# Statistics of a stage taken in the stage before it, and buffers filled one stage early, in an eight-stage kernel

## What is computed

```python
x = x + tanh(g_xattn[0]) * long_convolution(ctx, ctx, layernorm(x))
x = x + tanh(g_ffn[0])   * mixture_of_64_experts(layernorm(x))
x = x + tanh(g_xattn[1]) * rms_attention(layernorm(x), ctx)            # "second attention", 32 heads
x = x + tanh(g_ffn[1])   * mixture_of_8_experts_top_2(layernorm(x))    # "second mixture"
x = x + tanh(g_xattn[2]) * int8_attention(layernorm(x), ctx)           # "quantised attention"
x = x + tanh(g_ffn[2])   * int4_feed_forward(layernorm(x))
x = x + tanh(g_xattn[3]) * causal_attention(layernorm(x), ctx, ctx)
x = x + tanh(g_ffn[3])   * ternary_feed_forward(layernorm(x))
```

## Time and profile before

| | us |
|---|---|
| runs of the kernel before, median of 3 | 2333.38 |
| lowest and highest run | 2327.88, 2338.29 |
| the profiled execution, its own time | 2331.26 |
| its span, first to last instruction | 2329.5 |
| second attention, main loop | about 815 to 911 |
| second mixture | 911 to 1271 |
| quantised attention, first block; scoring loop | 1271 to about 1400; to 2004 |
| quantised feed-forward | 2004 to 2078 |
| causal attention | 2078 to 2227 |
| ternary feed-forward | 2227 to the end |

### The profile page before, as it was taken

How to read it: one execution, slowest core, us unless ns; L and a number is a source line. 1 busy time by engine, 2 the same in 40 slices (tenths; PEclk the granted TensorE clock), 3 DMA queues, 4 the chain that set the end, 5 groups by cost and what they waited for, 6 DMA issues and landing times. The chain is left out here.

```text
span 2329.5 us, 49096 instructions
## 1 busy us (share of the span) xinstructions
PE 1920.9 (82%) x17689; PEld 1096.4 (47%) x17713; DVE 1648.5 (71%) x2772; ACT 1344.6 (58%) x1832; POOL 893.1 (38%) x778
## 2 busy tenths in 40 slices
PE   3875999999997786899997778888888888558855
PEld 1343656656564464468874433333333333334533
DVE  4776765555555556853335889999999999457975
ACT  3444633333334675643332459999999999545566
POOL 4760000000001462500014447888888888334301
PEclk9776999999998898899999865555555555679989
DMA  6334221211222303513223116656666566120100
...
DMA packets 384868, 195.32 MB, mean 84 GB/s; under 512 B 312301, under 2 KB 355311, under 8 KB 382703
## 3 DMA queue, kind: packets, MB, share of 16 engines
...
## 5 line engine op out<-in xcount | busy, mean ns | idle before, releaser
L2455 POOL CAST qa_pT<-qa_eT 128x2048 bf16<-128x2048 uint8 x256 | 477.4, 1893 | 110.6 <-PE qa_OY L2481 95.0
L2568 ACT ACTIVATE qa_e<-qa_scores,qa_nb 128x2048 uint8<-128x2048 f32 x256 | 510.4, 1994 | 4.2
L2578 DVE TENSOR_SCALAR_CACHE_REDUCE qa_scores<-qa_S,qa_sq 128x1024 f32<-128x1024 f32 (+1 forms) x256 | 456.0, 1830 | 4.3 <-PE qa_S L2473 3.4
L2473 PE MATMUL qa_S<-qa_kT,qa_qT 32*128 32x512 f16 x1024 | 373.2, 615 | 95.6 <-DVE qa_scores L2578 94.3
L1116 POOL MEMSET rms_nothing<- 128x512 f16 x1 | 0.5, 524 | 579.8 <-POOLq L3486 579.8
L2473 PEld LDWEIGHTS qa_S<-qa_kT,qa_qT 32*128 32x128 f16 x1024 | 64.6, 108 | 310.2 <-DVE qa_scores L2578 267.0
L973 PE MATMUL moe_G<-hT,moe_W 128*128 (+1 forms) x792 | 193.7, 381 | 7.1 <-DVE moe_zero L941 7.1
L982 PE MATMUL moe_O<-moe_W,moe_ap 128*128 (+1 forms) x1584 | 194.5, 273 | 4.1 <-DVE moe_ap L937 4.1
L913 ACT ACTIVATE moe_ap<-moe_a 128x512 f16<-128x512 f32 x132 | 83.1, 629 | 194.6 <-DVE moe_a L935 194.6
L973 PE MATMUL moe_U<-hT,moe_W 128*128 (+1 forms) x792 | 192.7, 379 | 0.0
L982 PEld LDWEIGHTS moe_O<-moe_W,moe_ap 128*128 128x128 f16 x1584 | 154.7, 98 | 50.3 <-DVE moe_ap L937 3.9
...
## 6 DMA issues: line engine op xcount, KB each, us to landing
...
moe_W<-in_moe_w SPq DMA_DIRECT2D x40, 384.0 KB, 12.1
...
qa_eT<-qa_e SPq DMA_TRANSPOSE x256, 3.1
...
```

Of the source, the lines that this page charges most:

```text
L2455: nc.gpsimd.tensor_copy(pT[:, u % RING, :, :].rearrange("p (b r) q -> p b r q", r=2), pairs).then_inc(s_cast, 1)
L2473: last = nc.tensor.matmul(S[:, banks[i], :], qT[rows, g, t * P:(t + 1) * P], kT[rows, g, parts[i] * QW:(parts[i] + 1) * QW], start=True, s ...
L2568: nc.scalar.activation(e8[:, u % RING, :], scores[:, u % RING, :], ACT.Exp, bias=nb[:, p % 2, i:i + 1], accum_out=sums[:, u:u + 1]).then_i ...
L2578: nc.vector.tensor_scalar(target, S[:, banks[0]:banks[-1] + 1, :], sq[:, t, h:h + 1], so_far, ALU.mult, ALU.max, accum_out=greatest).then_ ...
```

## The change

Two small tiles, `sh.stats` and `sh.mv`, become shared by all stages. (1) The second attention's VectorE loop gets a `bn_aggr` and a `bn_stats` per row tile, for tiles that are finished, and a rest behind the loop; the second mixture starts at its square root. (2) The second mixture's last units get two `bn_stats` and two `bn_aggr` per unit from unit 72 on, and a rest behind `output(3)`; the quantised attention has no statistics of its own, and its four square roots stand first in ScalarE's list. (3) The causal attention's mask and its three stacks are allocated one stage earlier, by a new class, and filled there by GpSimd, which also makes the bf16 mask; ScalarE's copy of the mask and TensorE's waits for them are gone. The causal attention keeps its own statistics.

Two hunks that only declare `sh.stats`, `sh.mv` and a semaphore, and the shortened lists of semaphores, are left out here:

```diff
@@ -1383,6 +1386,14 @@
 
+                def next_statistics(t):
+                    dve.wait_ge(s_res, 2 * t + 2)
+                    nc.vector.bn_stats(sh.stats[:, t, :], sh.X[:, t, :]).then_inc(s_stats, 1)
+
+                def next_moments(t):
+                    dve.wait_ge(s_stats, t + 1)
+                    nc.vector.bn_aggr(sh.mv[:, t, :], sh.stats[:, t, :])
+
                 keys(0)
@@ -1392,7 +1403,14 @@
                     evacuate(t, 1)
+                    if t >= 2:
+                        next_moments(t - 2)
+                    if t:
+                        next_statistics(t - 1)
                 output(NB - 1, 1)
+                next_moments(NB - 2)
+                next_statistics(NB - 1)
+                next_moments(NB - 1)
 
@@ -1543,8 +1559,7 @@
             def _(act):
-                act.wait_ge(s_mv, NB)
-                nc.scalar.activation(std[:, :], mv[:, :, 1], ACT.Sqrt, bias=sh.eps[:, 0:1]).then_inc(s_std, 1)
+                nc.scalar.activation(std[:, :], sh.mv[:, :, 1], ACT.Sqrt, bias=sh.eps[:, 0:1]).then_inc(s_std, 1)
                 act.wait_ge(s_rw, 16)
@@ -1594,11 +1609,6 @@
                 chained = chain_on(dve, s_d)
-                for t in range(NB):
-                    nc.vector.bn_stats(stats[:, t, :], sh.X[:, t, :]).then_inc(s_stats, 1)
-                dve.wait_ge(s_stats, NB)
-                for t in range(NB):
-                    nc.vector.bn_aggr(mv[:, t, :], stats[:, t, :]).then_inc(s_mv, 1)
                 nc.vector.memset(L[:, :, NE:16], LOW)
@@ -1694,8 +1704,17 @@
 
+                def next_statistics(t):
+                    dve.wait_ge(s_comb, NB + t + 1)
+                    dve.wait_ge(s_res, t // 4 + 1)
+                    nc.vector.bn_stats(sh.stats[:, t, :], sh.X[:, t, :]).then_inc(s_stats, 1)
+
+                def next_moments(t):
+                    dve.wait_ge(s_stats, t + 1)
+                    nc.vector.bn_aggr(sh.mv[:, t, :], sh.stats[:, t, :])
+
                 positions()
-                done = 0
+                done, known = 0, 0
                 for i in range(UNITS):
@@ -1717,14 +1736,23 @@
                     if i >= LAST + 4:
+                        ended = min(done - NB, NB - 4)
                         for k in range(done, min(done + 3, 2 * NB)):
...
                         done = min(done + 3, 2 * NB)
+                        for t in range(known, min(known + 2, ended)):
+                            next_statistics(t)
+                            if t:
+                                next_moments(t - 1)
+                            known = t + 1
                 dve.wait_ge(s_D, UNITS)
...
                     combine(k)
-                dve.wait_ge(s_comb, 2 * NB)
+                for t in range(known, NB):
+                    next_statistics(t)
+                    next_moments(t - 1)
+                next_moments(NB - 1)
 
@@ -2218,8 +2244,7 @@
                     def deviations(c):
-                        act.wait_ge(s_mv, (c + 1) * Q)
-                        nc.scalar.activation(std[:, quarter(c)], mv[:, quarter(c), 1], ACT.Sqrt, bias=sh.eps[:, 0:1]).then_inc(s_std, 1)
+                        nc.scalar.activation(std[:, quarter(c)], sh.mv[:, quarter(c), 1], ACT.Sqrt, bias=sh.eps[:, 0:1]).then_inc(s_std, 1)
 
@@ -2252,11 +2277,11 @@
 
+                    for c in range(Q):
+                        deviations(c)
                     weights_high(wk, wkf, s_wk, 16, s_wkhi)
...
                         context_high(c)
-                    for c in range(Q):
-                        deviations(c)
                     weights_high(wv, wvf, s_wv, 32, s_wvhi)
@@ -2280,18 +2305,11 @@
 
-                    def statistics(c):
-                        for t in range(c * Q, (c + 1) * Q):
-                            nc.vector.bn_stats(stats[:, t, :], sh.X[:, t, :]).then_inc(s_stats, 1)
-                        dve.wait_ge(s_stats, (c + 1) * Q)
-                        for t in range(c * Q, (c + 1) * Q):
-                            nc.vector.bn_aggr(mv[:, t, :], stats[:, t, :]).then_inc(s_mv, 1)
-
                     def scales(c):
...
                         dve.wait_ge(s_rstd, c + 1)
-                        nc.vector.scalar_tensor_tensor(out=shift[:, quarter(c)], in0=mv[:, quarter(c), 0], scalar=-1.0, in1=rstd[:, quarter(c)],
+                        nc.vector.scalar_tensor_tensor(out=shift[:, quarter(c)], in0=sh.mv[:, quarter(c), 0], scalar=-1.0, in1=rstd[:, quarter(c)],
                                                        op0=ALU.mult, op1=ALU.mult).then_inc(s_shift, 1)
@@ -2337,10 +2355,7 @@
                     for c in range(Q):
-                        statistics(c)
-                        if c:
-                            scales(c - 1)
-                    scales(Q - 1)
+                        scales(c)
                     for p in range(PAIRS):
@@ -2608,7 +2623,7 @@
 
-def quantised_ffn(nc, sh, weights):
+def quantised_ffn(nc, sh, weights, next_buffers):
 
@@ -2645,6 +2660,7 @@
+                next_buffers.fill(pool)
@@ -2894,7 +2910,43 @@
 
-def causal_attention(nc, sh, a, gate, next_weights):
+class CausalBuffers:
+
+
+    SLOT, CW, NH, HD = 64, 32, 16, 16
+    PARTS = 3 * HD
+
+    def __init__(self, nc, ctx):
+        self.nc = nc
+
+        def sb(n, shape, dt=F32):
+            return ctx.enter_context(nc.sbuf_tensor("ca_" + n, shape, dt))
+
+        self.maskf = sb("maskf", [P, 2, 4, P])
+        self.mask = sb("mask", [P, 2, 4, P], BF16)
+        self.qs = sb("qs", [P, 4, self.NH, self.SLOT], F16)
+        self.ks = sb("ks", [P, 2, self.NH, self.SLOT], F16)
+        self.vx = sb("vx", [P, 4, self.NH, self.CW])
+        self.s_set, self.s_mask = (nc.alloc_semaphore(name="ca_" + n) for n in ("set", "mask"))
+
+    def fill(self, pool):
+        nc, maskf, s_set, s_mask = self.nc, self.maskf, self.s_set, self.s_mask
+        for tile in (maskf[:, :, :, :], self.qs[:, :, :, :], self.ks[:, :, :, :], self.vx[:, :, :, :]):
+            nc.gpsimd.memset(tile, 0.0).then_inc(s_set, 1)
+        pool.wait_ge(s_set, 4)
+
+        nc.gpsimd.affine_select(out=maskf[:, 0, :, :], in_=maskf[:, 0, :, :], compare_op=ALU.is_ge, fill=LOW,
+                                base=0, pattern=[[0, 4], [-1, P]], channel_multiplier=1).then_inc(s_mask, 1)
+
+        nc.gpsimd.affine_select(out=maskf[:, 1, :, :], in_=maskf[:, 1, :, :], compare_op=ALU.is_ge, fill=LOW,
+                                base=0, pattern=[[0, 4], [1, P]], channel_multiplier=-1).then_inc(s_mask, 1)
+        pool.wait_ge(s_mask, 2)
+        nc.gpsimd.tensor_copy(self.mask[:, :, :, :], maskf[:, :, :, :])
+        nc.gpsimd.memset(self.ks[:, :, :, self.PARTS:self.PARTS + 1], 1.0)
+        nc.gpsimd.memset(self.vx[:, :, :, self.HD:self.HD + 1], 1.0)
+
+
+def causal_attention(nc, sh, a, gate, next_weights, buffers):
 
@@ -2918,16 +2970,12 @@
-        maskf = sb("maskf", [P, 2, HALF, P])
-        mask = sb("mask", [P, 2, HALF, P], BF16)
+        mask, qs, ks, vx = buffers.mask, buffers.qs, buffers.ks, buffers.vx
-        qs = sb("qs", [P, 4, NH, SLOT], F16)
-        ks = sb("ks", [P, 2, NH, SLOT], F16)
-        vx = sb("vx", [P, 4, NH, CW])
@@ -2963,19 +3011,6 @@
             def _(pool):
-                nc.gpsimd.memset(maskf[:, :, :, :], 0.0).then_inc(s_set, 1)
-                nc.gpsimd.memset(qs[:, :, :, :], 0.0).then_inc(s_set, 1)
-                nc.gpsimd.memset(ks[:, :, :, :], 0.0).then_inc(s_set, 1)
-                nc.gpsimd.memset(vx[:, :, :, :], 0.0).then_inc(s_set, 1)
-                pool.wait_ge(s_set, 4)
-
-                nc.gpsimd.affine_select(out=maskf[:, 0, :, :], in_=maskf[:, 0, :, :], compare_op=ALU.is_ge, fill=LOW,
-                                        base=0, pattern=[[0, HALF], [-1, P]], channel_multiplier=1).then_inc(s_mask, 1)
-
-                nc.gpsimd.affine_select(out=maskf[:, 1, :, :], in_=maskf[:, 1, :, :], compare_op=ALU.is_ge, fill=LOW,
-                                        base=0, pattern=[[0, HALF], [1, P]], channel_multiplier=-1).then_inc(s_mask, 1)
-                nc.gpsimd.memset(ks[:, :, :, PARTS:PARTS + 1], 1.0).then_inc(s_set, 1)
-                nc.gpsimd.memset(vx[:, :, :, HD:HD + 1], 1.0).then_inc(s_set, 1)
                 for t in range(NB):
@@ -3033,8 +3068,6 @@
                         normalise(2 * c + 1)
-                act.wait_ge(s_mask, 2)
-                nc.scalar.activation(mask[:, :, :, :], maskf[:, :, :, :], ACT.Copy).then_inc(s_mask16, 1)
                 normalise(4)
@@ -3210,8 +3243,6 @@
 
-                pe.wait_ge(s_set, 6)
-                pe.wait_ge(s_mask16, 1)
                 queries_turned(0)
@@ -3514,10 +3545,11 @@
         with own_semaphores(nc):
-            quantised_ffn(nc, sh, quantised)
+            buffers = CausalBuffers(nc, ctx)
+            quantised_ffn(nc, sh, quantised, buffers)
         with own_semaphores(nc):
             ternary = TernaryWeights(nc, ctx, a)
-            causal_attention(nc, sh, a, sh.gates[:, 6:7], ternary)
```

(1 more changed line is left out.)

21 lines of the change are left out of this document (10 added, 11 removed).

## The result

Over 20 runs each the kernel after took 2324.25 us (2318.02 to 2330.65), the kernel before 2331.59 us (2326.38 to 2339.92). The ratio is 0.9962 with a 95% interval of 0.9953 to 0.9972. On 2331.59 us that is 8.9 us less, between 6.5 and 11.0 (the two medians themselves lie 7.3 us apart, inside that). That is a real gain, and it stays under the 0.5% that the prediction named as its bound. The forecast was a sum of -9.25 us and 2323.

What follows compares the result with a forecast made beforehand. No engine bounds the whole: time is the sum of eight barrier-separated stages, each with its own limit. Terms -4.65 - 2.5 - 2.1 = -9.25 us from 2332.3 give 2323 us, range 2315 to 2330.

Steps and rivals of the forecast that it cites:

- the 0.5%: Whole kernel: smallest difference a measurement can tell from no change, about 0.5% (11.7 us); most of the gain below it.
- Seam 1: Second attention to second mixture: start 5.3 us earlier, loop additions free, tail 0.65 us; together -4.65 us.
- rival (d): Second attention's loop: two added operations overrun the 0.75 us cover 15 times; slower, for example +15 us, 2347; chance 0.05.
- Rival (e): Second mixture's start: dense units wait for weight tiles, so the 5.3 us are lost; -4 us, 2328; chance 0.05.
- Seam 2, start: Quantised attention's start: first key product 8.5 us earlier, less waits behind GpSimd; gain 5.5 us (bounds 3.4 and 8.5).
- the eight `keys` follow back to back on VectorE, so the rest slides: Quantised attention's keys: VectorE sets the pace, so the 5.5 us gained at the first carry through.
- my bound of 3.4: Quantised attention's start: gain only 3.4 us if VectorE gets in only when GpSimd's whole run ends.
- Seam 2, end: Second mixture's end: last down product 0.95 us later, 2.0 us behind `output(3)`; together 3.0 us added.
- the 0.27 us a unit: Second mixture's last units: VectorE falls behind 0.27 us per unit over four units, as additions exceed 0.63 us idle time.
- Seam 3, causal attention: Causal attention's start: without fills and mask cuts there, `queries(0)` comes 3.3 us earlier (bounds 2.6 and 4.9).
- Seam 3, fills: Quantised feed-forward's start: GpSimd's fills may hold VectorE's `tensor_scalar`; cost 1.2 us, middle of 0 and 2.4.
- the good bounds of seam 2: Second mixture to quantised attention: with every bound on the good side, stated as -6.8 us; expected -2.5 us.

Runs made afterwards that it cites:

- Experiment 12: Spread fills kernel plus two unread bn_stats per tile in the second attention's loop; 2322.3 us in one execution, the kernel before 2328.2 beside it.
- seam 2 alone: Kernel before, with only the quantised attention's statistics moved into the second mixture's last units; ratio 0.9983 (0.9967 to 0.9999).
- the two pairs above: Changed kernel against seam 2 alone (first scores 106.35, 104.27 us); spread fills against those plus 64 identity transpositions starting the feed-forward (106.05, 99.53).
- experiment 1: Kernel before, with only the second mixture's statistics moved into the second attention's loop (seam 1 alone); ratio 0.9986 (0.9970 to 1.0002).
- set 1: Profiles on one chip: each seam alone on the kernel before (ratios 0.9986, 0.9983, 1.0006), and spread fills on the changed kernel (0.9955).
- experiment 3: Kernel before, with only the causal buffers' fills moved into the quantised feed-forward (seam 3 alone); ratio 1.0006 (0.9987 to 1.0025).
- experiments 5 and 6: Changed kernel with each fill waiting for the one ahead, or with a fifth unread fill; 2337.3 and 2342.8 us in one execution each.
- spread fills: Changed kernel with mask and cuts first, query and key stacks after the first rounding, value stack after the first down products; ratio 0.9955 (0.9941 to 0.9969).

## Why the prediction came out as it did

The total was right, -8.9 for -9.25 us, and two of the three seams did not come about as I had said. That the total fits so closely is luck: two errors cancel (below).

**Seam 1: as predicted.** -5.30 for the start (5.3), +0.68 for the tail (0.65), nothing in the loop (103.1 and 103.0 us). Experiment 12 puts two more `bn_stats` there and still gets no more than 0.2 us out of all 15 tiles; rival (d) was far off. Rival (e) is refuted: the mixture is shorter by the full amount.

**Seam 2, start: the step that failed is "the eight `keys` follow back to back on VectorE, so the rest slides".** Three things were off. First, the gain at `keys(0)` is 6.9 us and not 8.5: I took the end of one tile's product (1282.96) for the end of the pair that VectorE waits for. Second, the holds were mis-sized in the way of my bound of 3.4: the first `tensor_scalar` stood until GpSimd's whole run of low halves had ended, 3.71 us, so that 3.9 us were left (in three later profiles it stood for 1.1 to 1.7 us only). Third, and this is the failed step, VectorE does not bound the keys at the lower clock. There a pair of key products takes TensorE 3.85 us, against 3.11 on VectorE. In the changed kernel TensorE was at it for 20 us without a pause:

```profile
1286.16:1306.16 20.00, 20.00 (x85) 8.99 (x83) 17.97 (x34) 0.00 (x0) 10.59 (x12) 0.50 0.00 1
```

The lead of 3.9 us was 1.5 at the eighth key product, and gone (-0.1) at the next work on VectorE, 47.0 us behind the start. With seam 2 alone, where the clock rose 12.6 us earlier, the lead was 2.9 us at both places, and 1.8 at the first score. Over the profiles, the first score comes at 107.2 us on average where the stage takes its own statistics (four of them, 105.6 to 109.1) and at 104.3 where it does not (seven, 99.5 to 106.4, leaving out those with edits of their own in that part). So the start brought some 2.9 us, not 5.5. With so few profiles the standard error of that difference is about 1.2 us, so it is an estimate. Behind the keys VectorE's next work needs a transposition of TensorE, and VectorE idled 0.57 us for it in the changed kernel and not at all in the kernel before; so TensorE is the late one there. That the scatter up to the first score goes with the clock is shown by the two pairs above; no run sets the clock, so how much it cost in each is not measured.

**Seam 2, end:** +1.96 behind `output(3)` (2.0 predicted), 1.72 net to the next stage, and 0 for the last down product instead of 0.95. That product waits for VectorE as long as before, so the 0.27 us a unit did not add up. In the pair of profiles the mixture is 4.6 us shorter. Its start gives 5.3 and its tail takes 1.7; the other 1.0 us is the stretch at the lower clock 96 to 153 us behind its start (experiment 1), and not the change.

**Seam 3, causal attention:** -3.6 us for the start (3.3 predicted); the stage is 3.6 us shorter than in the two kernels of set 1 that lack the edit. In the pair of profiles before and after it is 2.1 us, with the clock up earlier in the kernel before (experiment 3).

**Seam 3, fills:** the middle of 0 and 2.4 was the wrong choice. Fills hold a `tensor_scalar`; the first transposition is 4.2 us late, beyond my upper bound, because I let VectorE in after the fill that was running. The Trainium skill (SBUF — State Buffer, "SBUF: two separate sides") has the port pair locked for the whole instruction, and its rule, which I had weighed, gave the right kind: an operation in a two-port mode collides with a fill, too. The size by it was 2.4 us; experiments 5 and 6 show that a run of ready fills can hold VectorE as if it were one. Yet the feed-forward is no longer for it: 73.9 us on average with the run of fills (two profiles), 73.9 without (three). The reason is seen only in part. In two of the three without, the granted clock fell in the middle of the stage, as in this row of the kernel with seam 1 alone, 38 to 49 us behind the stage's start; in the two with the fills it was 0.84 and 1.00 there.

```profile
2033.69:2044.69 11.00, 10.05 (x31) 5.59 (x32) 4.95 (x12) 3.21 (x5) 0.00 (x0) 0.53 0.00 0
```

Whether the late start keeps the clock up, or these five profiles just fell so, stays open; five profiles of one feed-forward with spread fills lie between 71.5 and 76.2 us.

**The sum.** With measured terms: -5.3 + 0.7 (seam 1), -2.9 + 1.7 (seam 2), -3.6 + 0 (seam 3) = -9.4, against -8.9 (-11.0 to -6.5). My terms were -4.65, -2.5 and -2.1; seam 2 gave 1.3 less than I had said and seam 3 gave 1.5 more, and these two errors cancel. Two slips of the prediction change nothing in it: the good bounds of seam 2 add up to -6.6 and not -6.8, and the scoring loop is a quarter of the time, not a third. The seams measured alone add up to -3.3 - 4.0 + 1.4 = -5.9 us, each with some 4 us either way, which agrees with the whole and decides nothing on a single seam. For seam 3 alone the -3.6 of the stages lies just outside the interval (-3.0 to +5.8), and I can't explain that.

**A version that beats both?** Spread fills at -10.5 us has the lowest ratio, but is not told apart from the change itself.
